# Attention layers on one core: first-attention tiles computed twice also where the plan has TensorE idle behind them

## The reference

```
x1  = layernorm(x + attn(x))      # 16 heads of 16; att = softmax(q k^T / 4) over all 2048 keys
out = layernorm(x1 + ffn(x1))     # route: mean over the rows of x1 @ Wr, the best 4 of 16 heads
# attn: opt = einsum('blmh,blhd->blhd', att, v), then @ w_out.T + b_out
# ffn:  O = softmax(Q K^T / 8) V for the 4 chosen heads of 64, then @ Wo + bo
```

## Time and profile before

| | before |
|---|---|
| median of the runs | 3879.66 us |
| the profiled execution's own time | 3876.35 us |
| its span, first to last instruction | 3874.3 us |
| busy: TensorE, VectorE, ScalarE, GpSimd | 3551.2, 3414.4, 3102.1, 1729.0 us |
| mean granted TensorE clock | 0.97 |
| matmuls of A tiles (L932) | 4838 |

### The profile page before, as it was taken

How to read it: one execution, slowest core, us unless ns; L and a number is a source line. 1 busy time by engine, 2 the same in 40 slices (tenths; PEclk the granted TensorE clock), 3 DMA queues, 4 the chain that set the end, 5 groups by cost and what they waited for, 6 DMA issues and landing times.

```text
span 3874.3 us, 43074 instructions
## 1 busy us (share of the span) xinstructions
PE 3551.2 (92%) x14510; PEld 1298.5 (34%) x14510; DVE 3414.4 (88%) x3380; ACT 3102.1 (80%) x5065; POOL 1729.0 (45%) x1262
## 2 busy tenths in 40 slices
PE   8999999789999999999999999899999999899997
PEld 3333333332222323433222323433222323343333
DVE  6999999989999989889999999889999999367776
ACT  4999999869999888888998988888998988523333
POOL 4233333304444346434444445434444445847665
PEclk9999999899999999899999999899999999999998
DMA  5222222200000001200000001200000000100000
GB/s 165 70 82 92 75 79 66 85 17 15 17 24 21 22 22 36 75 15 22 17 22 23 17 28 30 81 14 20 20 22 22 17 28 11 54 1 12 12 12 11
DMA packets 117198, 142.70 MB, mean 37 GB/s; under 512 B 33394, under 2 KB 100466, under 8 KB 116978
## 3 DMA queue, kind: packets, MB, share of 16 engines
q1 hardware_dynamic: 116978, 139.95, 11.9%
HBM read 89.55 MB, written 50.33 MB: 36 GB/s over the span
## 4 chain that ended last, share of the span: by engine, by line
PE 44%; DVE 33%; ACT 17%; issue 5%; POOL 1%; DMA 0%; SPq 0%; DVEq 0%; POOLq 0%; ACTq 0%
DVE nmax L1231 21%; ACT ps L1071 14%; PE ps L1029 10%; PE ps L932 9%; DVE smax L1320 7%; PE ps L994 7%; PE ps L1009 7%; PE ps L892 5%; PE ps L907 4%; PE ps L1044 1%; PE ps L1012 1%; DVE st L1208 1%; PE ps L901 1%; ACT part L1171 1%; ACT probs L1161 1%
## 5 line engine op out<-in xcount | busy, mean ns | idle before, releaser
L1231 DVE TENSOR_REDUCE nmax<-ps 128x1 f32<-128x1024 f32 x2048 | 2385.3, 1215 | 182.6 <-PE ps L932 176.3
L1071 ACT ACTIVATE ps<-ps,nmax 128x1024 f32<-128x1024 f32 x2048 | 2232.1, 1095 | 265.9 <-DVE nmax L1231 240.4
L932 PE MATMUL ps<-stack 96*128 96x512 bf16 x4838 | 1369.4, 391 | 192.4 <-ACT ps L1071 104.3
L848 POOL TENSOR_TENSOR facc<-facc,probs 128x1024 f32<-128x1024 f32 x443 | 1043.5, 2356 | 799.6 <-ACT probs L1161 723.3
L932 PEld LDWEIGHTS ps<-stack 96*128 96x128 bf16 x4838 | 355.7, 99 | 1324.0 <-ACT ps L1071 757.8
L1320 DVE TENSOR_REDUCE smax<-ps 128x2 f32<-128x1024 f32 x512 | 618.5, 1216 | 65.3 <-PE ps L994 64.5
L994 PE MATMUL ps<-fk,fq 64*128 64x512 f32 x2048 | 574.6, 643 | 39.4 <-ACT ps L1071 33.4
L1009 PE MATMUL ps<-fq,fk 64*128 64x512 f32 x2048 | 557.7, 624 | 16.4 <-DVE probs L1350 5.4
L1029 PE MATMUL ps<-probs,vals 128*64 128x512 f32 x2048 | 516.8, 611 | 5.9 <-DVE oT L1368 3.5
L1161 ACT ACTIVATE probs<-ps 128x1024 f32<-128x1024 f32 x384 | 391.4, 1019 | 77.7 <-PE ps L1012 77.3
L1071 ACT ACTIVATION_READ_ACCUMULATOR ps<-ps,nmax 128x1 f32 x2048 | 421.4, 206 | 0.0
(11 more groups left out here) (127 smaller groups left out, 2038.8 us busy)
## 6 DMA issues: line engine op xcount, KB each, us to landing
stack<-qk_levels SPq DMA_DIRECT2D x768, 64.0 KB, 2.2
qk_levels<-fk SPq DMA_DIRECT2D x64, 384.0 KB, 2.6
probs<-in_L_attn_x SPq DMA_DIRECT2D x16, 512.0 KB, 4.0
res<-in_L_attn_x SPq DMA_DIRECT2D x16, 512.0 KB, 4.5
v_rows<-vals SPq DMA_DIRECT2D x16, 512.0 KB, 2.7
vrows<-v_rows SPq DMA_DIRECT2D x16, 512.0 KB, 4.1
x_rows<-y SPq DMA_DIRECT2D x16, 512.0 KB, 3.0
res<-x_rows SPq DMA_DIRECT2D x16, 512.0 KB, 3.9
```

The costliest lines, as they stand in the source:

```text
L848: pool.tensor_tensor(total, total, probs[:, slot, :], ALU.add).then_inc(facc_ready, 1)
L932: last = pe.matmul(bank(banks[i]), stack[0:SK, hd % 2, 0, t * P:(t + 1) * P], stack[0:SK, hd % 2, 1, col:col + CH], start=True, stop=True)
L1071: act.activation(src, src, ACT.Exp, bias=nmax[:, b % 2, half, t, hd:hd + 1], scale=-1.0, accum_out=esum[:, b % 2, half, t, hd:hd + 1]).the ...
L1231: dve.tensor_reduce(nmax[:, b % 2, half, t, hd:hd + 1], two_banks(banks), AX.XY, ALU.min).then_inc(min_ready, 1)
```

## The change

It adds a second way into the set `again`. The plan now notes when each unit starts and ends in its own reckoning. When it is done, it adds each A tile behind which its TensorE is idle for more than `LEAST = 0.3` us until the next unit, in every batch, whatever stands near it and whether or not VectorE has a queue. The order, the banks and the costs in the plan stay as they are, since the set grows after the plan is finished.

```
+LEAST = 0.3
...
-    again = set()
+    again, spans = set(), {}
...
     def start(n, now, us):
         running[n[0]] = n
         order[n[0]].append(n)
+        spans[n] = (now, now + us)
         events.append((now + us, 0, rank[n], n))
...
+    again.update(n for n, m in zip(order["PE"], order["PE"][1:])
+                 if n[1] == "A" and spans[m][0] - spans[n][1] > LEAST)
```

## The result

The changed kernel took 3887.22 us (median of 12 runs), the kernel before 3879.55 us (12 runs on the same chips). The ratio is 1.0019, with a 95% interval of 1.0011 to 1.0027: 7.7 us slower, just inside the 0.2% that I called no change, and clearly not nothing. The forecast was 3882 us, range 3864 to 3912. The profiled execution took 3885.27 us, its span is 3883.4 against 3874.3.

What follows compares the result with a forecast made beforehand. VectorE and the ring of banks bind, TensorE has little to spare, and the clock is the second loss. Doubling costs +30.6, clock gives back 28.7: +1.9 on 3876.35 is 3878.3, plus 3.3 to the median, 3882 us (3864 to 3912).

Steps and rivals of the forecast that it cites:

- the tiles behind T: First-attention (A) tiles right after a transposed (T) tile, some 190 of the 450; said to be the ones that cost.
- The loop of 3.64 us a step: Middle stage, VectorE and banks: a doubled A tile behind T makes a step 3.64 us against 3.39, +0.25.
- the plain round: 25 stretches from one PV burst to the next, three tiles behind T in each: 0.44 x 25 = 11.0 us cost.
- FQ rounds: 15 rounds with an FQ projection, four tiles behind T in a row: 0.84 x 15 = 12.6 us cost.
- M rounds: Seven rounds with M transposes and no score tile (S) before them: 0.59 x 5 + 0.44 x 2 = 3.8 us cost.
- S ahead of M: Three rounds where A tiles, score tile S, M transposes and D matmuls follow each other: 12 of 14 us back.
- The A-only ends: Round ends of A tiles alone, some 130 tiles: doubling costs nothing; six clock falls behind them go, 11.7 us back.
- The clock, 28.7 back: Time regained from granted-clock falls: 11.7 us behind A-only ends, 12 with S ahead of M, 5 at seams; sum 28.7.
- The seams: Stretches between batches, low-clock time worth up to 25 us: 5 us back, between 5 lost and 15 won.
- M behind A: Four rounds with clock falls behind M and D with single A tiles (3.0+3.0+1.5+1.5 us): nothing given back.
- the rival that falls move rather than go: Steady rounds: stalls outweigh the clock, falls move to M and D or another phase; +30.6 us, 3910; chance 0.28.
- The page against the row: Steady rounds: page's long-gap rule returns no clock, +30.6 less at most 5 us; forecast followed the trace row on short gaps.

## Why the prediction was right

The range and the class held, and the mechanism in all its large parts; the centre was 5 us low, by terms that missed in both directions. A change of +1.9 was forecast and +7.7 came, so that it still counts as no change (the bound is 7.8) is luck.

- **A doubled tile costs 0.43 us, and only the tiles behind T are paid.** Shown by taking them out (3887 to 3854, each against its own kernel before) and by having only them (+28). The others cost next to nothing.
- **The loop of 3.64 us a step.** 3.59 to 3.70 us between doubled tiles, 4.02 or 4.03 with three passes for 3.97. Right.
- **Cost of 30.6 us.** It measured 35. Mis-sized term by term: the plain round 0.52 instead of 0.44 (25 rounds), FQ rounds 0.87 for 0.84 (15), M rounds 0.63 for 0.59 and 0.44 (7), and the "0.2 x 16" was 0.20 in eight and 0.40 in the eight with S ahead of M. With the behind-T tiles alone the sum comes out nearly as I had it: 0.43 to 0.44 a plain round, 0.21 with S ahead of M, 31.5 us in all. What I left out is that the two groups act on each other. I had let the first step of a row go free because 0.41 us stood behind its tile; the repeats at the ends make that tile 0.15 us later, 0.27 is left, and the repeat no longer fits. VectorE's idle time in the plain round grew by 0.3 us, not 0.4.
- **The A-only ends cost nothing.** By themselves, right in plain rounds: 23.69 us with them and without. The three rounds with the long stretch of A tiles take 24.17 us without a fall, 0.48 more. Whether that is a cost isn't shown. I had called these rounds equal in composition to the plain ones (26.2 against 23.7); their counts are equal, but their order is another, and no profile without the end tiles shows one without a fall.
- **The clock, 28.7 back.** The ends' 11.7 came whole, or 10.3 if the 0.48 isn't a cost. Of the 14 with S ahead of M all came, not 12. The seams gave 6, for 5, mostly the first.
- **M behind A: nothing.** This step failed. I took the four falls there as fixed. Eight came (seven in the second profile), 4.2 us more. The tiles behind T don't bring them: the two profiles with these alone have three and two such falls in the ten rounds, those of the kernel before four and three. Of the nine profiles with the end tiles eight have six to eight, the one with only the ends six; the ninth, with more work on both sides of M, has four. So the rival that falls move rather than go was right for this one kind of place, and the counts point to the repeats at the ends. Why is open.
- **The page against the row.** Doubling tiles with gaps of 0.4 to 0.6 us took away nine falls out of nine in two kinds of round. The Trainium skill's warning in TensorE: Matmul & The Clock Gate, section Why this matters for your kernels, is about long idle gaps. The measurement decides for the row. In the same page of the Trainium skill the section A second HAM failure mode: psum-queue depth-cycling tells of frequent short pauses between groups of matmuls, and these nine falls agree with it.
- **It does what it says.** Yes, 5738 matmuls. The groups hold 198, 150 and 102 tiles, where I had written 190, 130 and 130. The plan's idle time behind the tiles that follow a T was mostly 0.32 us; in the trace it was 0.24 or less behind 143 of the 198. Either is less than the 0.43 us that a repeat takes.

## What to carry to other kernels

In this kernel a repeated matmul was a fair way to hold the clock when it stood where the engine would have been idle anyway and where the reader wasn't waiting. Look at both the gap behind the tile and the time between its fill and its reader. Ask for a gap about as large as the repeat costs (0.43 us here) or larger: the threshold of 0.3 let in 204 tiles that took back more than the other 246 gave, and 0.4 turns 8 us lost into 26 us won. When a change moves little, look for rounds that got faster and rounds that got slower; here 32 us of gain were hidden under 41 us of loss. And filling the gaps of one stretch moves what comes after it: the repeats at the ends took 0.14 us from the gap of a tile further on, and more falls came in another kind of round.

## What I had not expected

- The number of falls differs between executions of one kernel: nine or six behind A-only ends, six or four of the long kind, while many of the places stay and every round without a fall repeats to 0.02 us. The spread of 27 us in one kernel's runs goes with it at least in part; single profiles count falls badly.
- The tiles behind T alone left more long falls than the kernel before had (six and four of eight rounds, against three and four). Why is open: nothing was changed in the stretch of A tiles ahead of these falls. Whether it is chance was not settled.
- In the long seam, ten us less at the low clock gave 1.1 us, 0.1 for each (0.2 from the kernel before to the changed one, 14 us for 2.9), against 0.43 to 0.46 in the rounds. TensorE is busy for 66 to 68 of these 72 to 74 us; what else the stretch waits for wasn't looked at.
